# Layer 0 of a two-layer transformer kernel: heads written out in slots, decay constants in PSUM, scores from f16 high and low parts

## What is computed

```python
# B=4 batches, T=512 tokens, C=512 channels; H=16 heads of 128
def step(carry, x):                       # forward, then the same in reverse
    a, b = carry
    a = a * decay + ekv_t                 # decay: one constant per channel
    b = b * decay + ek_t
num = nf + nb - ekv + euk * vf
den = df + db - ek + euk
base = sigmoid(r) * (num / max(den, 1e-08))
...
q, k, v = x @ Wq, x @ Wk, x @ Wv;  q, k = rope(q), rope(k)
s_full = q @ k.T * scale                  # causal
p_cmp = softmax(q @ mean(k, blocks of 64))
p_slc = softmax(where(slc_mask, s_full)); p_swa = softmax(where(window 64, s_full))
o = o_cmp * g_cmp + o_slc * g_slc + o_swa * g_swa
return o @ Wo
```

## Time and profile before

| | |
|---|---|
| time, median of 3 runs | 2350.09 us (2344.54 to 2351.07) |
| profiled execution | span 2350.2 us; no other time is given for it |
| busy, share of the span | TensorE 85%, VectorE 69%, ScalarE 57%, GpSimd 45% |
| granted TensorE clock, mean | 0.944 of full speed |
| instructions | 41986 |

### The profile page before, as it was taken

How to read it: one execution, slowest core, us unless ns; L and a number is a source line. 1 busy time by engine, 2 the same in 40 slices (tenths; PEclk the granted TensorE clock), 3 DMA queues, 4 the chain that set the end, 5 groups by cost and what they waited for, 6 DMA issues and landing times. The chain is left out here.

```text
span 2350.2 us, 41986 instructions
## 1 busy us (share of the span) xinstructions
PE 1995.9 (85%) x14177; PEld 1227.9 (52%) x14177; DVE 1613.1 (69%) x3496; ACT 1337.5 (57%) x3199; POOL 1053.6 (45%) x758
## 2 busy tenths in 40 slices
PE   0589988999999999999994579966689898968999
PEld 0355555665566655655652445534466666643444
DVE  7768777877877877866662359944676778753770
ACT  4576766666666566656553324425676767745442
POOL 5666666555556655544540246634332223210440
PEclk9999999999999999999996589987889999988999
DMA  4233332221122221221213954455433334425110
GB/s 176 86 106 102 100 103 92 97 77 67 62 88 97 68 76 60 72 93 61 74 51 135 377 204 148 144 197 158 130 118 118 109 122 136 135 103 193 41 36 22
DMA packets 110015, 260.51 MB, mean 111 GB/s; under 512 B 10672, under 2 KB 39472, under 8 KB 107824
## 3 DMA queue, kind: packets, MB, share of 16 engines
q1 hardware_dynamic: 90320, 208.85, 26.2%
q10 hardware_dynamic: 16992, 41.43, 5.1%
q0 software_dynamic: 2560, 8.39, 1.0%
HBM read 179.46 MB, written 76.02 MB: 109 GB/s over the span
## 5 line engine op out<-in xcount | busy, mean ns | idle before, releaser
L830 PE MATMUL ps_q<-a_y,a_w 128*128 128x512 f16 x1536 | 344.0, 381 | 0.0
L625 POOL TENSOR_TENSOR a_rb<-a_rb,a_rot 128x512 f32<-128x512 f32 x129 | 193.5, 1500 | 284.1 <-ACT a_rb L736 283.6
L830 PEld LDWEIGHTS ps_q<-a_y,a_w 128*128 128x128 f16 x1536 | 148.4, 98 | 177.2 <-issue 3.1
L848 PE MATMUL ps_s<-a_kk,a_q 128*128 128x512 f32 (+3 forms) x512 | 190.2, 481 | 26.2 <-POOL a_kk L629 26.2
L270 DVE TENSOR_TENSOR_SCAN wkv_bwd<-wk_decay,wkv_tail,wkv_fwd 128x512 f32<-128x512 f32 x114 | 202.2, 1798 | 0.1
L883 PE MATMUL ps_g<-a_o,a_wo 128*128 (+1 forms) x768 | 178.0, 382 | 10.3 <-POOL a_o L616 7.9
L837 PEld LDWEIGHTS ps_v<-a_w,a_y 128*128 128x128 f16 x3072 | 176.9, 98 | 15.1
L837 PE MATMUL ps_v<-a_w,a_y 128*128 128x128 f16 x3072 | 182.0, 219 | 0.0
L872 PE MATMUL ps_o<-a_tt_,a_v 128*128 128x512 f32 (+3 forms) x512 | 160.2, 457 | 16.0 <-ACT a_tt_ L756 13.4
L735 ACT ACTIVATE a_rb<-ps_q 64x512 f32<-64x512 f32 x129 | 76.6, 593 | 169.3 <-DVE a_ra L958 167.3
L972 DVE TENSOR_REDUCE a_nmax<-ps_s 128x1 f32<-128x512 f32 (+3 forms) x256 | 125.4, 490 | 64.3 <-PE ps_s L850 60.5
(11 more groups left out here) (286 smaller groups left out, 4769.0 us busy)
## 6 DMA issues: line engine op xcount, KB each, us to landing
a_w<-wqkv_split SPq DMA_DIRECT2D x48, 768.0 KB, 4.3
scratch_numlog<-wkv_nl ACTq DMA_DIRECT2D x40, 512.0 KB, 2.7
wkv_kt<-in_fT ACTq DMA_DIRECT2D x58, 256.0 KB, 2.6
a_wraw<-in_wqkv SPq DMA_DIRECT2D x18, 768.0 KB, 5.3
wqkv_split<-a_w SPq DMA_DIRECT2D x17, 768.0 KB, 6.8
a_stacks<-qk_parts SPq DMA_DIRECT2D x96, 128.0 KB, 2.5
gate_up<-in_gate_up SPq DMA_DIRECT2D x8, 1408.0 KB, 16.1
a_nlc<-scratch_numlog SPq DMA_DIRECT2D x18, 512.0 KB, 4.7
```

Of the source, the lines that this page charges most:

```text
L625: pool.tensor_tensor(rb[:, n, :], rb[:, n, :], rot[:, 2 * n + 1, :], ALU.mult).then_inc(s["roped"], 1)
L830: mm = pe.matmul(psq[n][:], w16[:, i % 2, wp, n, c, :], y16[b % 2][:, yp, c, :], start=c + m == 0, stop=c == CC - 1 and m == 2)
L848: pe.matmul(cols(ps, j, -lead), q[:, j * P:(j + 1) * P], kk[:, NBLK - lead:NBLK + P * (j + 1)], start=True, stop=False)
```

## The change

Layer 0's heads are written out without loops as 66 slots (`LAST`). In slot p TensorE does the scores of head p-2, v of head p-1, q and k of head p, one piece of output for the group that ended, and then the transposes (`turn`) and values of head p-2. The other engines follow the same slots. The front's units keep the raw exponentials, sums and logs in PSUM banks that the heads use later; `psg` is gone (gates and output go to `psv`), and its bank, `psd`, holds a copy of the 64 decay constants per partition, which the scans read, and the four maxima `cmax`. q and k are split into f16 halves (`q16`, `k16`, two buffers of each), and the scores are three products of these. Wo is split in 16 pieces instead of four, half of them in the front and half in slots 2 to 11. The transfers at the start are issued in another order.

```diff
     def raw(self, u):
+        if self.in_front(u):
+            return self.front["raw"]
         return self.ek_raw[u % self.raws if self.raws > 1 else 0]
+
+    def forward_sums(self, u):
+        return self.front["fwd"] if self.in_front(u) else self.fwd
+
+    def backward_sum(self, u, m):
+        return self.front["bwd"][m] if self.in_front(u) else self.bwd[:, m, :]
...
-    def decay(self, b, n):
-        return self.constant("decay", b, n).to_broadcast([P, T])
+    def dve_take_decays(self, dve):
+
+        dve.tensor_copy(self.decays, self.k.wkv["decay"][:]).then_inc(self.s["decays"], 1)
+        dve.wait_ge(self.s["decays"], 1)
+
+    def decay(self, b, n, apart=True):
+
+        if self.decays is None or not apart:
+            return self.constant("decay", b, n).to_broadcast([P, T])
+        one = self.decays[:, bass.ds(b, 1), bass.ds(n, 1)].rearrange("p a n -> p (a n)")
+        return one.to_broadcast([P, T])
...
-        dve.tensor_tensor_scan(self.bwd[:, m, ::-1], self.decay(b, n), self.fwd[:, m, ::-1], self.tail[:, m:m + 1],
+        dve.tensor_tensor_scan(self.backward_sum(u, m)[:, ::-1], self.decay(b, n, not self.in_front(u)),
+                               self.forward_sums(u)[:, m, ::-1], self.tail[:, m:m + 1],
                                ALU.mult, ALU.add).then_inc(s["back"], 1)
...
+        wkv = Wkv(k, ctx, "wkv0", 2, PER, decays=psd[:, 0:DECAYS],
+                  front={"units": CC, "raw": psv, "fwd": banks[:, 0:2, :], "bwd": [psq[0][:], psq[1][:]]})
...
+                def qk_low(g):
+                    pool.wait_ge(s["q_hi"], g + 1)
+                    pool.tensor_tensor(q16[:, g % 2, 1], q[:], q16[:, g % 2, 0], ALU.subtract).then_inc(s["qk_lo"], 1)
+                    pool.wait_ge(s["k_hi"], g + 1)
+                    pool.tensor_tensor(k16[:, g % 2, 1], kk[:], k16[:, g % 2, 0], ALU.subtract).then_inc(s["qk_lo"], 1)
...
+                def qk_high(g):
+                    act.wait_ge(s["q_sb"], g * 2 + 1)
+                    if g >= 2:
+                        act.wait_ge(s["scores"], (g - 2) * 3 + 3)
+                    act.activation(q16[:, g % 2, 0], q[:], ACT.Copy).then_inc(s["q_hi"], 1)
+                    act.wait_ge(s["ksum"], g + 1)
+                    act.activation(k16[:, g % 2, 0], kk[:], ACT.Copy).then_inc(s["k_hi"], 1)
...
                 def scores(g):
-                    pe.wait_ge(s["q_sb"], g * 2 + 2)
+                    pe.wait_ge(s["qk_lo"], g * 2 + 2)
                     for bank, tiles in BANK_TILES0:
-                        if bank == 1:
-                            pe.wait_ge(s["ksum"], g + 1)
                         for j in tiles:
                             lead = NBLK if bank else 0
-                            pe.matmul(cols(ps, j, -lead), q[:, j * P:(j + 1) * P], kk[:, NBLK - lead:NBLK + P * (j + 1)],
-                                      start=True, stop=False)
+                            for m, (qp, kp) in enumerate(PARTS):
+                                pe.matmul(cols(ps, j, -lead), q16[:, g % 2, qp, j * P:(j + 1) * P],
+                                          k16[:, g % 2, kp, NBLK - lead:NBLK + P * (j + 1)], start=m == 0, stop=False)
...
-                run(pe, group, last)
+                for p in range(LAST):
+                    b, it, i = slot_of(p)
+                    if p % H0 == 2 and p < HEADS:
+                        gates(b)
+                    if p >= 2:
+                        scores(p - 2)
+                    if 1 <= p <= HEADS:
+                        if output_of(p - 1) is not None:
+                            pe.wait_ge(s["acc"], output_of(p - 1) + 1)
+                        if p % H0 == 2:
+                            pe.wait_ge(s["gates_step"], b * 2 + 1)
+                        project_v(p - 1)
+                    if p < HEADS:
+                        project(p)
+                    if output_of(p) is not None:
+                        pe.wait_ge(s["v_sb"], min(p, HEADS))
+                        output(output_of(p))
+                    if p >= 2:
+                        turn(p - 2)
+                        values(p - 2)
```

More of the change, by code:

```diff
@@ L473, in run @@
-        def run(eng, group, last, after_first=lambda: None):
-            group(0, 0, True, False)
-            with eng.Fori(1, CC) as c:
-                group(0, c, False, False)
-            after_first()
-            for b in range(1, B):
-                group(b, 0, True, True)
-                with eng.Fori(1, CC) as c:
-                    group(b, c, False, False)
-            last()
-        def opening(b):
-            return isinstance(b, int) and b == 0
-        def final(b):
-            return isinstance(b, int) and b == B - 1
@@ L540, in store @@
                 def store(b, co):
[L541 to L560 removed]
+                    sp.wait_ge(s["acc"], (b * CC + CC - 1) * CC + co + 1)
@@ L669, in _ @@
-                rope(0, 0)
-                run(pool, group, lambda: o_low(B * H0 - 1, (B * CC - 1) % 2, G - 1))
+                split(0)
+                for c in range(1, CC):
+                    wkv.pool_prepare(pool, c % 2, c)
+                    wo_low(2 * c - 2)
+                    y_low(0, c - 1)
+                    wo_low(2 * c - 1)
+                    if c == 1:
+                        split(1)
+                y_low(0, CC - 1)
+                for m in range(2 * CC - 2, 2 * G):
+                    wo_low(m)
@@ L886, in output @@
                     mm.then_inc(s["out_ps"], 1)
-                def group(b, c, first, output_before):
-                    it = b * CC + c
-                    og, oc = (it + 1) % 2, (c + (CC - 1)) % CC
-                    for i in range(G):
-                        g = b * H0 + c * G + i
-                        before = output_before or not first
-                        if first and i == 0:
-                            if output_before:
-                                pe.wait_ge(s["acc"], (it - 1) * CC + 1)
-                            gates(b)
-                        project(b, g, i, 16 * pairs(b, c, i))
-                        if i and before:
-                            output(it - 1, og, oc, i)
-                        if i or before:
-                            values(g - 1, i + G - 1)
-                        scores(g)
-                        if i == 0 and before:
-                            if first:
-                                pe.wait_ge(s["gates_sig"], b + 1)
-                            output(it - 1, og, oc, 0)
@@ L1062 @@
+                for n in range(output_of(LAST), GROUPS * CC):
+                    output(n)
 EARLY = 6
```

649 lines of the change are left out of this document (356 added, 293 removed).

## The result

| | before | after |
|---|---|---|
| median of 4 runs | 2348.7 us (2344.5 to 2351.1) | 2253.1 us (2249.8 to 2257.3) |
| profiled span | 2350.2 us | 2248.1 us |
| first projection of layer 0 | 82.6 us | 57.2 us |
| end of layer 0's last output | 1264.8 us | 1163.12 + 2.76 = 1165.9 us |
| instructions | 41986 | 40165 |

The ratio is 0.9589 (95% interval 0.9574 to 0.9604). Of the 102 us between the two profiled spans, 99 lie in layer 0; 25 of them were won in the front.

A forecast was written before the change was run, and what follows sets the result against it. TensorE was taken to bound layer 0's heads, VectorE's softmax path coming second. First projection at 58 plus 1117 us ends the last output at 1175 instead of 1264.8, 90 us less: 2260 us, range 2235 to 2290 (8 in 10: 2215 to 2315).

The forecast's parts named there:

- slots 16 to 63 with gates: Batches 1 to 3 of layer 0: gates 7, eight groups 533, batch 3 262 us.
- slots 64, 65 and last outputs: End of layer 0: two softmax-bound slots without a projection, 29 us, then four last outputs with waits, 18 us.
- The front: Before layer 0's first projection: VectorE's work undisturbed 9.1 us a chunk, 1 us allowed for logs; first projection from 82.6 to 58.
- Decay in PSUM: Layer 0's scans: with the decay constant in PSUM they are free of GpSimd and take 1.2 us, bounds 1.2 and 2.2.
- The slow rival: Layer 0's scans stay at 2.2 us despite decay in PSUM, lengthening slots and front: 2374 us, chance 0.05.
- Scores: TensorE's score matmuls: three f16 products instead of f32 take 2.04 us a head against 2.80, bounds 1.9 and 2.8.
- The wait at values: Slots i = 0 and 2: ScalarE's copies queue behind the swap, so TensorE's values wait; 1.2 us charged to each.
- the first rival: Values in layer 0's slots don't wait, as ScalarE swaps before TensorE arrives: 2215 us, chance 0.15.
- the sum of VectorE's path: VectorE's softmax in slots with forward scans, first maximum to window terms: 12.3 us, nearly tying with TensorE's 12.49.
- Slot 2: Third slot of the opening, charged 17.9 us like the others of slots 2 to 15.
- The opening behind slot 2: Rest of batch 0, where weights are also split: 17.9 us a slot, chosen between 16.04 and 19.37.
- Cover for the halves: Copies and subtractions making f16 halves: ScalarE 11.9, GpSimd 11.8, VectorE 13.2 us per head, hidden beside TensorE's 16.04.

The follow-up runs named there:

- e1: Changed kernel with every scan of layer 0 reading its decay constant from SBUF again instead of PSUM: 2311.0 us, ratio 0.9821.
- e5: Changed kernel with slots 0 and 1 reordered: head 0's low halves ahead of GpSimd's join, the sigmoid's log behind ScalarE's swaps: 2248.7 us, ratio 0.9567.
- e2: Changed kernel with scores as one f32 product per tile again, without the copies and subtractions for f16 halves: 2282.2 us, ratio 0.9719.
- e7: Changed kernel with two score products instead of three (low half of q with high half of k left out): 2247.4 us, ratio 0.9551.
- e12: Changed kernel with slots 0 and 1 reordered, gates of batches 1 to 3 a slot earlier, and the condition's prepare behind the rope steps: 2248.8 us, ratio 0.9568.
- e6: Kernel before with the three f16 score products alone, halves made right behind k's rotation, no extra slot of distance: 2661.6 us, ratio 1.1311.

## Why the prediction was right, and which terms were off

| step | predicted | measured |
|---|---|---|
| first projection | 58 | 57.2 |
| slots 0 and 1 | 17 | 74.22 - 57.17 = 17.1 |
| slots 2 to 15 | 251 | 340.29 - 74.22 = 266.1 |
| slots 16 to 63 with gates | 7 + 533 + 262 = 802 | 1120.87 - 340.29 = 780.6 |
| slots 64, 65 and last outputs | 29 + 18 = 47 | 1165.9 - 1120.87 = 45.0 |
| last output ends | 1175 | 1165.9 |

A slot is counted as in the prediction: it opens with TensorE's scores, or with the wait for them.

- **The front**: the size was right. Its reason held in kind: a trace shows VectorE's long holds of the earlier trace rows gone (four forward products' scans 13.4 us before, 4.9 after). Putting either the decays or the sums back costs 4 us, not 25; both together were not put back. What else went is GpSimd's subtraction of Wo, 4 instructions of 4.1 to 5.0 us before, 1.15 us apiece after. That these long ones made the long holds is read from the timelines: the scan of 5.01 us runs from 32.71 to 37.72, the subtraction beside it from 31.69 to 36.65, and in `e1`, where the front's scans have two SBUF inputs again beside the short pieces, no VectorE instruction there is longer than 2.28 us. Neither the pieces nor the other order of loads was tried alone, so what won the rest of the 25 us stays open.
- **Decay in PSUM**: 1.2 us taken, 1.21 to 1.28 measured. The slow rival's price, 78 us in 12 groups, 20 in the opening and 16 in the front, was too high: it measured 30 (3.8 a group in batches 1 and 2, nothing in batch 3), 19.4 and 4.1 (`e1`).
- **Scores**: 2.04 taken, 1.96 measured.
- **The wait at values**: mis-sized. I charged 1.2 us to slots 0 and 2; it is 0.26 where the gates are far, and such a slot is 0.15 us longer than the others (16.17 against 16.02), so batches 1 to 3 came out 21 us shorter. There the first rival, no wait at values, was nearer than the forecast. The failed step is the sum of VectorE's path, 12.3 us: the timeline of a slot i = 2 shows 11.3.

```profile
440.00 0.81 PE L925 MATMUL ps_s<-a_k,a_q 128*128 128x512 f16 x3
...
444.75 1.21 DVE L275 TENSOR_TENSOR_SCAN wkv_fwd<-ps_d,wkv_ek 128x512 f32<-128x512 f32 x1
...
448.17 1.93 DVE L1091 SCALAR_TENSOR_TENSOR a_pt<-ps_s,a_coef,a_pc 128x512 f32<-128x512 f32 x4
...
451.25 1.28 DVE L1046 TENSOR_TENSOR a_ra<-ps_q,a_rot 128x512 f32<-128x512 f32 x2
...
452.41 1.26 PE L943 MATMUL ps_s<-ident,a_pt 128*128 128x128 f32 x10
...
453.19 1.36 ACT L819 ACTIVATE a_tt_<-ps_s 128x512 f32<-128x512 f32 x3
```

  The window terms end when the rope steps start, 451.25 - 440.00 = 11.25 us after the scores. Every term was a little too long. From start to start the coefficients take 0.92 us for 1.21 (in the earlier trace rows they hold VectorE's waits of 0.21 and 0.16 us, for ScalarE and for its own step before), the first part 3.26 for 3.54, the scans 2.50 for 2.65, the other four 0.05 to 0.10 less each. The order of events was as predicted (rope, swap, copies, values).
- **Slot 2**: mis-sized by 15 us. I charged it 17.9 us like the slots behind it, and it took 107.25 - 74.22 = 33.0: it is the first with scores and a softmax. TensorE waits for k's low half and then for the first p, and the granted clock is 0.50 from 76.3 to 86.4 and from 96.8 to 106.8 us. The timeline shows what was queued in front of k's low half: ScalarE's log waits for its chunk ahead of the first swap, and GpSimd's join ahead of the subtraction.

```profile
64.93 0.63 ACT L737 ACTIVATE a_sg<-a_xc 128x512 f32<-128x512 f32 x1 [9.10 <-DMA a_xc<-in_xT]
...
73.89 1.45 POOL L233 TENSOR_TENSOR wkv_nl<-wkv_bwd,wkv_eukv 128x512 f32<-128x512 f32 x1
...
78.16 1.60 POOL L667 TENSOR_TENSOR a_q<-a_q 128x512 f16<-128x512 f32 x1
...
80.94 1.46 PE L925 MATMUL ps_s<-a_k,a_q 128*128 128x512 f16 x3 [6.72 <-POOL a_k L669]
...
100.67 2.40 PE L943 MATMUL ps_s<-ident,a_pt 128*128 128x128 f32 x10 [7.11 <-DVE a_pt L1098]
```

  `e5` confirms the cause of the 6.7 us: without it the scores start 6.9 us sooner. It also shows that this order alone brings 4 of the 15 us.
- **The opening behind slot 2**: 17.9 a slot taken, 233.0/13 = 17.9 measured. The figure was chosen between two bounds and not worked out, so this is luck. `e2` shows that the opening is 6 us shorter without the halves.
- **Cover for the halves**: "all below 16.04, so this work lies beside TensorE's" held for the busy time. It left out that a slot is a ring of engines, which `e7` shows to be within 1 us a group of TensorE.

The mis-sized terms cancelled in part: +15 (slot 2) against -21 (slots 16 to 63), -2 (the end) and -1 (the front). That 2260 came so near to 2253 is in part luck.

## What to carry to other kernels

A shorter matmul is worth its difference only where its operands are ready a stage ahead: the same products cost 127 us without a slot of distance (and a second buffer) and brought 30 with it. Before shortening the busiest engine, follow the ring of the other engines once around (join, limit, softmax, rope, swap, copies); with it within 1 us, 0.55 us a slot taken off TensorE made a group longer. Constants that a VectorE instruction reads beside a second SBUF operand belong in PSUM if GpSimd works at the same time.

## What the runs showed of the hardware

- A broadcast [128, 1] constant in SBUF makes a scan an instruction with two SBUF inputs: 2.23 us beside GpSimd against 1.27 from PSUM, and GpSimd's own products grow as well (1.57 against 1.28 us).
- What kept two SBUF inputs is still held. The condition, in 345 to 1126 us, before and after; it now runs beside GpSimd's sine product (453.22 and 453.24 us in one slot):

```profile
L289 DVE SCALAR_TENSOR_TENSOR a_yf<-wkv_nl,wk_fomd,a_sg 128x512 f32<-128x512 f32 x9 | 6.7, 742 | 0.0
```

```profile
L314 DVE SCALAR_TENSOR_TENSOR a_yf<-wkv_nl,wk_fomd,a_sg 128x512 f32<-128x512 f32 x8 | 12.5, 1567 | 0.0
```

  It stands behind the rope steps, off the way to the transposes; what it costs was not tried. A window term on that way was held in `e12`: 2.40 us for 0.41, until 0.2 us after the end of GpSimd's 3.09 us.
- A wait of TensorE can cost twice: behind 3.64 us of idling, values ran at a granted clock of 0.50 (4.64 us for 2.43, `e6`), and the first scores of the changed kernel, also at 0.50, took 1.46 us for 0.81 behind their 6.72 us.
